# A two-layer decoder on one core: the context's keys and values of the second attention are computed during the recurrent mixer

## The chip, the cores and the metric

One core of a Trainium2 chip runs the whole program in one launch. The metric is device time in microseconds (us) of that core, the median of several executions. TensorE (PE in the profile, with PEld for its weight loads) multiplies and transposes, VectorE (DVE), ScalarE (ACT) and GpSimd (POOL) do the rest, SyncE (SP) only issues transfers (DMAs). Each engine works off its own queue in order; a semaphore wait at the head of a queue holds everything behind it. Everything is 32-bit float but a few counting steps.

## The reference

`x` and `ctx_1024` have 16 sequences of 128 rows, 256 wide. Two layers, each of mixer, attention over the context, mixture of experts, each with a residual and a plain layer norm:

```python
x = _layernorm(x + L0_attn(x))              # state space mixer
x = _layernorm(x + L0_xattn(x, ctx, ctx))   # 16 heads of 16
x = _layernorm(x + L0_ffn(x))               # 16 banks, 2 per row
x = _layernorm(x + L1_attn(x))              # recurrent mixer (wkv) with its own gated feed-forward
x = _layernorm(x + L1_xattn(ctx, x))        # 8 heads of 64, below
x = _layernorm(x + L1_ffn(x))               # 32 experts, 6 per row, one shared, 16 anchors
```

The second attention is the one changed:

```python
xn = layer_norm(ctx, gamma_x, beta_x);  ln = layer_norm(x, gamma_l, beta_l)
q = (ln @ Wq) * 64 ** -0.5
k_x, v_x = split(xn @ Wkv);  k_l, v_l = split(ln @ Wkv)
k = concat([rope_rotate_k(k_x), k_l]);  v = concat([v_x, v_l])
out = softmax(q k^T) v @ Wo                 # per sequence and head: 128 queries, 256 keys
```

What the change moves is `xn`, `k_x` (with the rotation) and `v_x`: they depend on the context alone.

## The kernel before, in words

`X` holds the residual stream, a batch (one sequence) on 128 partitions by 256. `Engine` objects T, V, A, G, S record the queue of each engine; a call's `w=` puts waits on handles ahead of it. `Slots` is a ring of buffers, each with the handles that free it; `ps` is the ring of the 8 PSUM banks. A part of the kernel is a generator that yields where another part's instructions may come in between. `pipeline` starts one generator per step and advances every live one by one segment in each step, the oldest first; so the order in each engine's queue is fixed at build time.

Stages, in order: state space mixer; first attention (16 batches in groups of four, `pre_c` making queries, keys and values of a group, `post_c` closing it, the function `fill` called three times a batch to advance them); first routing; 47 tiles of experts (`tile0`, 41 of them always); the recurrent mixer (`phase_e`, 8 units of two batches); second attention; second routing spread through it; experts and anchors; the final sum.

- `comb0(u)`, the head of `phase_e(u)`: four gathers by GpSimd of expert rows, two batches' sums on VectorE, a layer norm. Segment by segment a unit then does: scale and affine, the three mixes (VectorE), three projections, two scans and a reciprocal of 512 (VectorE), an output projection, a layer norm, the feed-forward of 1024 (TensorE), two layer norms. A unit takes 13 steps; the unit that runs step 6 has the scans.
- `fill_zeros` issues, on SP's queue, one of 50 blocks of zeros of some 2.2 MB into the destinations `xs` and `xsa` of the second routing, with three lanes, so that SP stops at a block until the third before it has landed. 24 are issued in the first attention; the mixer issues the other 26, up to four calls a unit. `place`, deep in the second attention, waits for all.
- `pre_f(g)`: loads the context of four batches on SP's queue (`in_ctx`), scales `x` on ScalarE and turns it into `lt`, then layer norm of the context (bn_stats on VectorE, a power on GpSimd, ScalarE applies it), turns it (8 transposes) into the other half of `lt`; then queries and the keys of `x`, one 512-wide product pair per segment.
- `keys_f(g, b)`: keys of the context (two 512-wide products), the rotation (two VectorE products out of PSUM, one GpSimd sum), values of context and of `x` (two products each, copies on ScalarE), then four transposes of the keys and a copy on ScalarE.
- `half_f(g, b, hf)` does the scores, maximum, exponential, transposes and values of four heads; `post_f` the output projection and the routing (`choose_f`, `place`: 7 scatters by GpSimd per batch, two between yields). Items come in the order `keys_f` of the next batch, half 0, `post_f` of the last, half 1, with `pre_f` of the next group in each group's first batch.
- The arena (53,200 columns of each partition) is laid out anew per stage; barriers stand between stages.

## Time and profile before

| | us |
|---|---|
| median of 3 runs | 1767.93 |
| lowest, highest | 1762.32, 1769.79 |
| profiled execution, its own time | 1781.69 |
| its span (first to last instruction) | 1779.9 |

| engine | busy us | share of the span |
|---|---|---|
| PE | 1437.8 | 81% |
| DVE | 846.7 | 48% |
| ACT | 571.7 | 32% |
| POOL | 516.8 | 29% |

The mean granted clock of TensorE is 0.903 of full speed. Busy time is a mean over stages with different limits; in the trace the first attention lies at 160 to 340 us, the first experts at 398 to 694, the recurrent mixer at 696 to 976, the second attention at 977 to some 1430, its last part routing alone.

### The profile page before, as it was taken

To read this page: it belongs to the slowest core of one execution; us is meant where nothing else is said; L and a number is where in the kernel's file an instruction comes from. 1 tells how busy PE (TensorE), PEld (TensorE's weight loads), DVE (VectorE), ACT (ScalarE), POOL (GpSimd) and SP (SyncE) were. 2 spreads that over 40 slices of the span, in tenths; PEclk is the share of its full clock that TensorE was granted. 3 is DMA by queue.
4 is the path that set the end of the run, shared out by engine and by line. 5 is a ranking of instruction groups with operands and counts; after the bars stand their busy time and mean duration, and the time that the engine had idled before them with its cause. 6 is when DMAs were issued, how large, how long until landed. Compare 5 with 4: busy or idle time off the path is not lost.

```text
span 1779.9 us, 30995 instructions
## 1 busy us (share of the span) xinstructions
PE 1437.8 (81%) x11425; PEld 1145.6 (64%) x11425; DVE 846.7 (48%) x2403; ACT 571.7 (32%) x1448; POOL 516.8 (29%) x524
## 2 busy tenths in 40 slices
PE   8567888649999997568997789978886467999878
PEld 4454676539999996346886356645555245888767
DVE  6254565451112222698852145555675433555534
ACT  3222322222222221123222254555454212555520
POOL 1011000011111102444443001034255634556544
PEclk9898999769999998678999799999997767999989
DMA  7745776649888881999999100011012596455456
GB/s 168 116 159 183 316 287 275 266 148 375 331 325 327 330 322 65 198 224 224 214 213 212 33 13 1 13 37 48 25 60 70 224 345 215 148 150 151 143 207 239
DMA packets 154926, 329.22 MB, mean 185 GB/s; under 512 B 11936, under 2 KB 118064, under 8 KB 149264
## 3 DMA queue, kind: packets, MB, share of 16 engines
q1 hardware_dynamic: 135424, 277.34, 51.6%
q0 software_dynamic: 15888, 43.52, 7.0%
q10 hardware_dynamic: 3456, 6.29, 1.1%
q8 instruction: 94, 1.54, 0.4%
q14 instruction: 64, 0.52, 0.1%
HBM read 174.51 MB, written 152.60 MB: 184 GB/s over the span
## 4 chain that ended last, share of the span: by engine, by line
PE 50%; DVE 12%; issue 5%; ACT 5%; POOL 4%; DMA 4%; DVEq 0%; SPq 0%; ACTq 0%; another core or an unknown queue 0%; POOLq 0%
PE bank L153 50%; DVE arena L153 11%; ACT arena L153 5%; POOL arena L153 3%; POOL xs L153 1%; DMA arena<-ys,arena 1%; DMA arena<-in_bank 1%; DMA arena<-xsa 1%; DMA arena<-in_ctx 1%; DVE arena L130 0%; DMA arena<-in_banka 0%; DMA xs<-arena 0%; DVEq L129 0%; POOL xsa L153 0%; DMA arena<-ys 0%
## 5 line engine op out<-in xcount | busy, mean ns | idle before, releaser
L153 PE MATMUL bank<-arena 128*128 128x128 f32 (+11 forms) x11425 | 1437.8, 326 | 336.1 <-DVE arena L153 151.7
L153 PEld LDWEIGHTS bank<-arena 128*128 128x128 f32 (+7 forms) x11425 | 1145.6, 175 | 628.0 <-issue 239.4
L153 ACT ACTIVATE arena<-bank 128x512 f32<-128x512 f32 (+3 forms) x627 | 267.5, 465 | 637.5 <-PE bank L153 591.9
L153 POOL TENSOR_TENSOR arena<-arena 128x512 f32<-128x512 f32 (+5 forms) x180 | 176.7, 982 | 719.3 <-DVE arena L153 563.1
L153 ACT ACTIVATE arena<-bank,arena 128x256 f32<-128x256 f32 (+3 forms) x486 | 204.0, 455 | 233.0 <-PE bank L153 154.4
L153 DVE TENSOR_TENSOR arena<-bank,arena 128x128 f32<-128x128 f32 (+5 forms) x331 | 123.8, 388 | 177.7 <-PE bank L153 101.6
L153 DVE TENSOR_SCALAR arena<-bank,arena 128x128 f32<-128x128 f32 (+1 forms) x212 | 69.7, 384 | 268.5 <-PE bank L153 268.5
L153 ACT ACTIVATE arena<-arena 128x256 f32<-128x256 f32 (+9 forms) x203 | 107.5, 586 | 270.5 <-DVE arena L153 244.8
L153 POOL DMA_INDIRECT ys<-arena x146 | 152.2, 1043 | 135.6 <-ACT arena L153 84.3
L153 DVE COPY arena<-bank 128x256 f32<-128x256 f32 (+2 forms) x136 | 76.4, 579 | 141.8 <-PE bank L153 139.5
L153 DVE TENSOR_REDUCE arena<-bank 128x4 f32<-128x512 f32 (+1 forms) x128 | 81.0, 684 | 91.4 <-PE bank L153 91.3
L153 POOL DMA_INDIRECT xs<-arena x96 | 95.0, 989 | 64.8 <-ACT arena L153 33.1
L153 DVE SCALAR_TENSOR_TENSOR arena<-arena 128x1 int32<-128x1 f32 (+4 forms) x297 | 87.3, 314 | 51.0 <-POOL arena L153 16.9
L153 POOL DMA_INDIRECT arena<-xd,arena x41 | 38.8, 947 | 250.1 <-PE bank L153 219.7
L153 DVE TENSOR_TENSOR arena<-arena 128x512 f32<-128x512 f32 (+18 forms) x248 | 98.6, 422 | 6.0
L130 DVE COPY arena<-arena 128x768 f32 x114 | 65.1, 571 | 48.3 <-issue 28.8
L153 DVE TENSOR_SCALAR arena<-arena 128x2 f32<-128x2 f32 (+12 forms) x178 | 49.0, 278 | 25.2 <-POOL arena L153 18.1
L153 DVE BATCH_NORM_STATS2 arena<-arena 128x6 f32<-128x256 f32 x128 | 48.6, 419 | 11.9 <-DMA arena<-in_ctx 9.4
L153 DVE RECIPROCAL arena<-arena 128x4 f32<-128x4 f32 (+8 forms) x56 | 38.4, 686 | 26.5 <-ACT arena L153 24.2
L153 POOL DMA_INDIRECT arena<-ys,arena x32 | 33.5, 1048 | 8.8 <-issue 8.8
L153 DVE RECIPROCAL arena<-bank 128x256 f32<-128x256 f32 x16 | 28.1, 1755 | 14.3 <-PE bank L153 14.3
L153 ACT ACTIVATION_READ_ACCUMULATOR arena<-bank,arena 128x1 f32 x128 | 26.1, 204 | 0.0
(22 smaller groups left out, 146.5 us busy)
## 6 DMA issues: line engine op xcount, KB each, us to landing
arena<-in_bank SPq DMA_DIRECT2D x41, 2052.0 KB
xs<-arena SPq DMA_DIRECT2D x32, 2193.0 KB, 31.8
xsa<-arena SPq DMA_DIRECT2D x16, 2193.0 KB, 9.7
arena<-xs SPq DMA_DIRECT2D x114, 129.0 KB
arena<-ys SPq DMA_DIRECT2D x16, 896.0 KB, 6.8
arena<-in_bank SPq DMA_DIRECT2D x8, 1536.0 KB, 6.8
arena<-kd SPq DMA_DIRECT2D x16, 512.0 KB, 10.3
arena<-in_banka ACTq DMA_DIRECT2D x24, 256.0 KB
```

The lines of the kernel that those rows point to most:

```text
L130: eng.tensor_copy(out, src[:, bass.ds(at * size, size)]).then_inc(self.sem, 1)
L153: ins = fn(*a, **kw)
```

## The change

In the first attention each group's context, which is there anyway, is also normalised (without gamma and beta) and stored to a new tensor `cnd`. Near the end of the first experts a part `fetch` loads its first two pieces of 256 rows on ScalarE's queue. `context(u)`, 8 of them, turns a piece and makes rotated keys and values of its two batches in one buffer `ob` of 1024 columns; `turn_keys` transposes the keys, and stores the buffer (512 KB) to `kvd` from ScalarE's queue. The mixer's loop is written out: before the live units advance, `tick()` runs twice in steps 0 to 4 and once in later ones; one tick stands before the mixer's gathers. A tick starts a unit of context at every even count and advances the live ones. There are two buffers `ob` (in `XT`), so that a batch's rotation waits for the store of the batch two before. In the second attention `load_kv` fetches keys and values of a batch, two batches ahead, on SP's queue, and waits for all stores; `pre_f` and `keys_f` lose the context's part. The mixer's ring `mix` has 8 buffers instead of 9.

```diff
         def layernorm(src, dst, nb, w=(), act=False, again=None):
             V.wait(*w, *sw)
+            if act:
+                A.wait(*w)
...
+        def norm_c(g):
+            cb, hc = C[g]["ctx"]
+            nb, w = cnb.get()
+            V.wait(hc)
+            h = yield from layernorm(lambda b: cb[:, b * 256:(b + 1) * 256], lambda b: nb[:, b * 256:(b + 1) * 256], 4, w=w, act=True)
+            ctxb.put(cb, h, C[g]["turned"])
+            if g + 2 < 4:
+                load_c(g + 2)
+            yield
+            h_cn.append(S.dma(s.dma_start, cnd[512 * g:512 * g + 512, :].rearrange("(b t) f -> t b f", b=4), view(nb, 0, [[256, 4], [1, 256]]), nlane, w=[h]))
+            cnb.put(nb, h_cn[-1])
+            yield
...
             if pre and slot[0] % 3 != 2:
                 next(pre, None)
+            if slot[0] % 3 == 2:
+                next(norm, None)
...
+        def load_cn():
+            u = len(loaded)
+            if u < 8:
+                cb, w = cbuf.get()
+                loaded.append((cb, A.dma(a.dma_start, view(cb, 0, [[256, 2], [1, 256]]), cnd[256 * u:256 * u + 256, :].rearrange("(b t) f -> t b f", b=2), cnl[u % 2], w=[*h_cn, *w])))
+
+        def context(u):
+            cb, hc = loaded[u]
+            ct, cw = cnT.get()
+            for kc, bk, h in to_feature(lambda b, kc: cb[:, b * 256 + kc * 128:b * 256 + kc * 128 + 128], [hc], 2):
+                hl = A(a.activation, ct[:, kc * 256:kc * 256 + 256], bank(bk)[:, 0:256], ACT.Identity, scale=vcol("gx", kc), bias=vcol("bx", kc), w=[h, *cw])
+                ps.put(bk, hl)
+            cbuf.put(cb, h)
+            load_cn()
+            yield
+            for b in range(2):
+                ob, ow = kvo.get()
+                bk, bw = ps.get()
+                T.wait(hl, h_w[3], *h_late, *bw)
+                for kc in range(2):
+                    h = mm(bank(bk), ct[:, kc * 256 + b * 128:kc * 256 + b * 128 + 128], wcol("kv2", kc, 0, 512), kc == 0, kc == 1, sig=(kc == 1))
+                rb, rw = rope.get()
+                V(v.tensor_tensor, view(rb, 0, [[64, 8], [1, 64]]), view(bank(bk), 0, [[64, 8], [1, 64]]), view(cc("cos"), 0, [[0, 8], [1, 64]]), ALU.mult, w=[h, *rw, *ow], free=True)
+                h = V(v.tensor_tensor, view(ob, 0, [[64, 8], [32, 2], [1, 32]]), view(bank(bk), 32, [[64, 8], [-32, 2], [1, 32]]), view(cc("sin"), 0, [[0, 8], [32, 2], [1, 32]]), ALU.mult, free=True)
+                ps.put(bk, h)
+                hr_ = G(p.tensor_tensor, rb, rb, ob[:, 0:512], ALU.add, w=[h])
+                bk, bw = ps.get()
+                T.wait(*bw)
+                for kc in range(2):
+                    h = mm(bank(bk), ct[:, kc * 256 + b * 128:kc * 256 + b * 128 + 128], wcol("kv2", kc, 512, 512), kc == 0, kc == 1, sig=(kc == 1))
+                hv = A(a.activation, ob[:, 512:1024], bank(bk), ACT.Copy, w=[h, *ow])
+                ps.put(bk, hv)
...
+                turning.append((2 * u + b, ob, rb, hr_))
+                yield
+                turn_keys()
+            yield
+
+        def turn_keys():
+            n, ob, rb, hr_ = turning.pop(0)
+            bk, bw = ps.get()
+            T.wait(hr_, *bw)
+            for m in range(4):
+                h = tr(bank(bk)[:, m * 128:(m + 1) * 128], rb[:, m * 128:(m + 1) * 128], ident, sig=(m == 3))
+            rope.put(rb, h)
+            hk = A(a.activation, ob[:, 0:512], bank(bk), ACT.Copy, w=[h, hr_])
+            ps.put(bk, hk)
+            h_kv.append(A.dma(a.dma_start, kvd[128 * n:128 * n + 128, :], ob, kvl[n % 2], w=[hk]))
+            kvo.put(ob, h_kv[-1])
+
+        def tick():
+            if ticks[0] % 2 == 0 and ticks[0] < 16:
+                units.append(context(ticks[0] // 2))
+            ticks[0] += 1
+            units[:] = [c for c in units if next(c, "end") != "end"]
...
-        pipeline([tile0(i) for i in range(LIKELY0)])
+        pipeline([tile0(i) for i in range(LIKELY0 - 4)] + [fetch()] + [tile0(i) for i in range(LIKELY0 - 4, LIKELY0)])
...
+        tick()
         for e in (T, V, A, G):
             e.wait(*h_ys[-3:])
...
-        mix = Slots([alloc(512) for _ in range(9)])
+        mix = Slots([alloc(512) for _ in range(8)])
...
-        pipeline([phase_e(u) for u in range(8)])
+        live, todo, n = [], deque(phase_e(u) for u in range(8)), 0
+        while todo or live:
+            for _ in range(2 if n < 5 else 1):
+                tick()
+            if todo:
+                live.append(todo.popleft())
+            live = [e for e in live if next(e, "end") != "end"]
+            n += 1
...
         def pre_f(g):
-            hc = S.dma(s.dma_start, view(cb, 0, [[256, 4], [1, 256]]), cv[g], clane2[0], w=cw)
-            h = yield from layernorm(cg, cg, 4, w=[hc], act=True)
-            for kc, bk, h in to_feature(lambda b, kc: cb[:, b * 256 + kc * 128:b * 256 + kc * 128 + 128], [h]):
-                hl = A(a.activation, lt[:, 1024 + kc * 512:1024 + kc * 512 + 512], bank(bk), ACT.Identity, scale=vcol("gx", kc), bias=vcol("bx", kc), w=[h])
...
+        def load_kv():
+            n = len(got_kv)
+            if n < 16:
+                kv, w = KV.get()
+                got_kv.append((kv, S.dma(s.dma_start, kv[:, 0:1024], kvd[128 * n:128 * n + 128, :], clane2[n % 5], w=[*h_kv, *w])))
...
         def keys_f(g, b):
-            rb, rw = rp.get()
-            hr = G(p.tensor_tensor, rb[:, 0:512], rb[:, 0:512], rb[:, 512:1024], ALU.add, w=[h])
-            for src in range(2):
...
+            load_kv()
+            c["kv"], c["hkx"] = got_kv[4 * g + b]
+            yield
             for kc in range(2):
+                h = mm(bank(bk), lt[:, kc * 512 + b * 128:kc * 512 + b * 128 + 128], wcol("kv2", kc, 512, 512), kc == 0, kc == 1, sig=(kc == 1))
+            c["hv"] = A(a.activation, c["kv"][:, 1024:1536], bank(bk), ACT.Copy, w=[h, c["hkx"]])
...
-        items = [pre_f(0)] + [nothing() for _ in range(7)] + [keys_f(0, 0)] + [nothing() for _ in range(6)]
+        items = [pre_f(0)] + [nothing() for _ in range(3)] + [keys_f(0, 0)] + [nothing() for _ in range(4)]
```

## Rows read from the trace of the kernel before

**Rows 1.** Stretches: us, then busy (count) per engine, PE clock, DMA share, GB/s.
```profile
160.00:340.00 180.00, 146.69 (x2743) 117.61 (x2741) 102.54 (x214) 57.80 (x120) 10.11 (x6) 0.94 0.76 298
694.00:735.00 41.00, 14.59 (x37) 10.67 (x38) 20.08 (x54) 5.74 (x14) 24.05 (x29) 0.54 0.55 132
735.00:821.00 86.00, 52.64 (x206) 41.98 (x205) 75.59 (x143) 19.78 (x42) 39.33 (x39) 0.78 1.10 224
821.00:971.00 150.00, 145.46 (x689) 127.02 (x687) 87.19 (x171) 41.38 (x80) 64.38 (x64) 1.00 1.10 214
977.00:1035.00 58.00, 39.29 (x149) 20.81 (x150) 15.96 (x43) 21.91 (x50) 4.56 (x4) 0.79 0.12 31
1035.00:1378.00 343.00, 290.03 (x1854) 192.18 (x1854) 191.45 (x559) 170.92 (x445) 106.89 (x110) 0.92 0.10 34
1378.00:1430.00 52.00, 21.40 (x80) 10.93 (x78) 25.48 (x108) 11.71 (x20) 32.78 (x34) 0.70 0.57 211
```

**Rows 2.** Chain of waits, shares by line, for 735 to 821 and 1035 to 1378.
```profile
by line: DVE arena L153 77.0%; PE bank L153 10.5%; POOL arena L153 4.9%; issue 4.4%; ACT arena L153 3.2%; DVEq L140 0.2%
...
by line: PE bank L153 55.6%; DVE arena L153 22.8%; ACT arena L153 12.7%; issue 6.1%; POOL xsa L153 1.3%; POOL xs L153 1.2%; POOL arena L153 0.2%; ACTq L140 0.1%; DVEq L140 0.1%; POOLq L140 0.0%
```

**Rows 3.** Groups by shape, 977 to 1380: count, busy us, mean ns, idle before.
```profile
L153 PE MATMUL bank<-arena 128*128 128x512 f32 x320 | 156.2, 620 | 0.9 <-ACT arena L153 0.9
L153 ACT ACTIVATE arena<-bank 128x512 f32<-128x512 f32 x148 | 83.5, 601 | 117.9 <-PE bank L153 115.7 <-issue 1.8
L153 DVE TENSOR_TENSOR arena<-bank,arena 128x512 f32<-128x512 f32 x32 | 20.5, 683 | 3.4 <-PE bank L153 3.4
L153 POOL TENSOR_TENSOR arena<-arena 128x512 f32<-128x512 f32 x16 | 20.3, 1268 | 93.7 <-DVE arena L153 93.7
```

**Rows 4.** Timeline of PEld, head of second attention: start, us, [idle before].
```profile
996.91 0.34 PEld L153 LDWEIGHTS bank<-arena 128*128 128x128 f32 x1 [0.52 <-issue]
...
1001.01 0.19 PEld L153 LDWEIGHTS bank<-arena 128*128 128x128 f32 x1 [0.24 <-issue]
```

**Rows 5.** Timeline of PE in the second attention.
```profile
992.21 1.97 PE L153 MATMUL bank<-arena 128*128 128x128 f32 x8 [11.74 <-ACT arena L153]
...
1025.27 2.22 PE L153 MATMUL bank<-arena 128*128 128x128 f32 x16 [1.33 <-DVE arena L153]
...
1116.00 47.95 PE L153 MATMUL bank<-arena 128*128 128x128 f32 x286 [4.00 <-ACT arena L153]
```

**Rows 6.** Timeline of DVE: the context's statistics, and the mixer's first scan.
```profile
734.57 1.22 DVE L153 TENSOR_TENSOR_SCAN arena<-arena 128x512 f32<-128x512 f32 x1
...
986.65 1.41 DVE L153 BATCH_NORM_STATS2 arena<-arena 128x6 f32<-128x256 f32 x4 [9.43 <-DMA arena<-in_ctx]
```

**Rows 7.** Landing times: mixer's gathers 696 to 735, 735 to 800; then `in_ctx`.
```profile
DMA to landing us min/median/max: 2.7/5.6/8.8
...
DMA to landing us min/median/max: 8.1/9.1/10.2
...
DMA to landing us min/median/max: 3.8/5.0/9.3
```

**Rows 8.** SP's queue in the mixer, and the page's issues of `xs` (median landing last).
```profile
712.34 252.25 SPq L153 DMA_DIRECT2D xs<-arena  x24
...
xs<-arena SPq DMA_DIRECT2D x32, 2193.0 KB, 31.8
```

**Rows 9.** Timeline of POOL: first gather, third unit's first scatter, last scatter.
```profile
699.26 0.95 POOL L153 DMA_INDIRECT arena<-ys,arena  x1 [0.16 <-issue]
...
1334.74 1.27 POOL L153 DMA_INDIRECT xsa<-arena  x1 [1.24 <-ACT arena L153]
...
1428.01 0.96 POOL L153 DMA_INDIRECT xs<-arena  x1 [0.30 <-issue]
```

**Rows 10.** Groups by shape, first attention 160 to 340.
```profile
L153 ACT ACTIVATE arena<-arena 128x256 f32<-128x256 f32 x12 | 6.2, 588 | 10.3 <-DVE arena L153 10.3
L153 DVE BATCH_NORM_STATS2 arena<-arena 128x6 f32<-128x256 f32 x12 | 4.2, 414 | 0.1
```

More of the change, by code:

```diff
@@ L642, in pre_c @@
                 ps.put(bk, hct)
-            ctxb.put(cb, h)
-            if g + 2 < 4:
-                load_c(g + 2)
+            c["turned"] = h
             yield
@@ L856, in build @@
                 pre, slot[0] = (pre_c(g + 1) if g < 3 else None), 0
+                norm = norm_c(g)
             m, hm = maxima(g, b)
@@ L1062, in tile0 @@
             yield
-        pipeline([tile0(i) for i in range(LIKELY0)])
+        kvd = nc.dram_tensor("kvd", [2048, 1024], F32, kind="Internal").ap()
+        cbuf = Slots([arena[:, 48848 + 512 * i:49360 + 512 * i] for i in range(2)])
+        cnT = Slots([arena[:, 49872 + 512 * i:50384 + 512 * i] for i in range(2)])
+        kvo, rope = Slots([]), Slots([])
+        cnl, kvl = [Lane(sem()) for _ in range(2)], [Lane(sem()) for _ in range(2)]
+        h_kv, loaded, turning = [], [], []
+        def load_cn():
[3 more added lines that the diff above has]
+                loaded.append((cb, A.dma(a.dma_start, view(cb, 0, [[256, 2], [1, 256]]), cnd[256 * u:256 * u + 256, :].rearrange("(b t) f -> t b f", b=2), cnl[u % 2], w=[*h_cn, *w])))
@@ L1065, in build, with fetch @@
+        ticks, units = [0], []
+        def tick():
[3 more added lines that the diff above has]
+            units[:] = [c for c in units if next(c, "end") != "end"]
+        def fetch():
+            yield
+            load_cn()
+            load_cn()
+        pipeline([tile0(i) for i in range(LIKELY0 - 4)] + [fetch()] + [tile0(i) for i in range(LIKELY0 - 4, LIKELY0)])
         with where_more(counts[0:1, 0:1], LIKELY0, NT0, r["hn"]):
@@ L1123, in build @@
         th = Slots([alloc(512) for _ in range(2)])
+        for i in range(2):
+            kvo.put(XT[:, 2048 + 1024 * i:3072 + 1024 * i])
+            rope.put(alloc(512))
         none = alloc(ROWX)
+        assert top[0] <= 48848
         V(v.memset, none, 0.0, free=True)
@@ L1309, in build @@
         oT2 = Slots([alloc(512) for _ in range(2)])
-        clane2 = [Lane(sem())]
+        clane2 = [Lane(sem()) for _ in range(5)]
         F = [dict() for _ in range(4)]
@@ L1397, in half_f @@
             c, f = FB[4 * g + b], F[g]
-            q, keys = f["q"], ((c["kx"], 128, 0), (f["kl"], 512, b * 128))
+            q, keys = f["q"], ((c["kv"], 128, 0), (f["kl"], 512, b * 128))
             m_, mw = sm.get()
@@ L1410, in half_f @@
             if hf:
-                kx.put(c["kx"], *hs)
                 if b == 3:
@@ L1457, in half_f @@
             if hf:
-                V2.put(vb, h)
+                KV.put(c["kv"], h)
                 c["ot"], tw = oT2.get()
@@ L1611, in post_f @@
                     yield
-        items = [pre_f(0)] + [nothing() for _ in range(7)] + [keys_f(0, 0)] + [nothing() for _ in range(6)]
+        for _ in range(2):
+            load_kv()
+        items = [pre_f(0)] + [nothing() for _ in range(3)] + [keys_f(0, 0)] + [nothing() for _ in range(4)]
         last = None
```

57 lines of the change are left out of this document (17 added, 40 removed).

## The prediction, made before the result was known

> **What bounds the kernel now.** I read first the stretches of time [rows 1]: they tell which engine is full where the change takes from and where it puts. In the second attention (1035 to 1378) PE is busy 290 of 343 us; in the mixer's second half (821 to 971) 145 of 150 at full clock. In the mixer's first half (735 to 821) DVE is busy 76 of 86 and PE 53, at a granted clock of 0.78; ahead of that (694 to 735) PE works 15 of 41 us at 0.54. So the room is in the mixer's first 125 us, and the second half has none. The chain of waits says the same [rows 2]: 77% DVE in 735 to 821; in the second attention 56% PE, 23% DVE and 13% ACT, so that PE work removed there isn't all time. Last, the timeline of POOL: it scatters from 1334.7 to 1429 with hardly a pause, while PE ends its last attention work near 1378 [rows 9]; whatever the last blocks gain is kept by the scatters. And the DMA engines are full through the mixer (share 1.10, 214 to 224 GB/s, against 34 in the attention) [rows 1].
>
> **What is moved, in TensorE time.** A batch's context costs 4 products of 512 columns (two for keys, two for values) and 4 transposes; a group 8 transposes more. The trace has each product as two records (320 where the code has 160) [rows 3]; from one weight load to the next are 0.43 us at full clock and 0.86 at half [rows 4]. A product is then 0.86 or 1.72 us. Transposes: 16 in 2.22 us at full clock, 8 in 1.97 at half [rows 5], 0.14 and 0.25 each. Sum: 64 x 0.86 + 96 x 0.14 = 68 us at full clock. DVE moves 32 rotations of 0.68 (22 us), POOL 16 sums of 1.27 (20 us), ACT 32 copies of 0.60 (19 us) [rows 3], each to the same number of instructions in the mixer.
>
> **Second attention, head.** The statistics of the first context wait 9.4 us for its load and start at 986.65 [rows 6]. PE has turned `x` by 980.5, then stands idle for 11.7 and turns the context in 2.0 [rows 5]; the products come only behind that. After the change they need the turned `x` alone: 13.7 us earlier. In front of the first scores two key and value pairs (3.4 us), 4 transposes and their waits also go, about 5. Saved: 18, if the first keys are there (see below).
>
> **Second attention, body.** Per group 4 x (3.44 + 0.56) + 1.1 = 17 us of PE go. In the ten steps with `pre_f` PE runs without a gap (48 us from 1116 [rows 5]); about 2.5 batches' keys and the context's transposes lie there, 11 us, and they go whole: what is left (37 us in ten steps, 3.7 a step) is more than the exponential and maximum ask per step on ACT and DVE (171 and 191 of 343 us, half of each [rows 1]). In the other seven steps PE's gaps are for DVE and ACT; of 6 us of PE there I count 2.5, and 1.5 for two copies and two rotations less in front of other work, 4 together. A group: 15. Groups 0 and 1 count whole, the third up to its third batch (12): 42. From there POOL's scatters bind; they lose only their sums of 1.27, and ACT and DVE hold them a little less: 5. Body 47, bounds: 30, if only the full-PE stretches give, to 68, all of the PE time less nothing. `load_kv` issues run two batches ahead of their use, some 40 us, against landings of 3.8 to 9.3 for as many bytes [rows 7]: no cost. Together 65 us less (48 to 85).
>
> **First attention.** `norm_c` adds per group 4 statistics of 0.41, small steps, a power on POOL, and 4 ACT passes of 0.59 [rows 10]: about 2.7 us DVE, 2.4 ACT, placed after the powers of every batch. PE is busy 147 of 180, DVE 103, ACT 58 [rows 1]. DVE is needed for the next maxima only after PE has made them, so most is hidden: 4 us in all (0 to 20, the upper end is all of it on the path). The later load of context g+2 still has some three batches of time. `fetch` and the tick ahead of the gathers stand beside full weight loads and the wait for the last stores: 0.
>
> **Mixer, steps 0 to 4, two ticks each.** Before, they took from 696.2 to the first scan at 734.6 [rows 6], 38 us, mostly waiting for gathers. I put the ticks into the queues one by one. In step 0 the keys' product (3.4 us at half clock, or 1.7), rotation 1.4, POOL's sum 1.3, then the same for the second batch stand ahead of the gathers on POOL: they start near 707 to 710, not 699.3 [rows 9], 10 late. In each later step: a transpose and copy, store issue, product, rotation; the second tick's rotation waits for the store issued in the first, since there are two buffers. PE needs 8.5 us a step (17 at half clock), the store 4 to 9, as `in_ctx` of the same bytes [rows 7], so a step is some 11 to 13 us against 7.7 before. In step 4 the fills stand beside it. Step 5 begins 28 us later: first scan near 763 (bounds +12, if the work fits the gathers' waits, to +50, if PE stays at half clock).
>
> **Steps 5 to 10, one tick each.** A step is about 20 us here and DVE's. A tick adds rotations of 1.4 and up to 1 of waiting for the product: five of them, 11 us; the products lie in PE's gaps, and PE's own products on the chain speed up with the clock (0.78 to 1.00), back 3. The last two batches fall into the full-PE half: 2 x 4 = 8. Sum 16 (5 to 25). Buffers: the store of a batch has a whole step of 20 us before its buffer is wanted. `mix` with 8 holds two steps of four: 0. Mixer together +44 (20 to 75).
>
> The price of a store beside the fills is the unknown. The gathers, 128 KB, land in 5.6 us with few fills and in 9.1 among them [rows 7]; the fills in 31.8 [rows 8] at 2193 KB, three in flight. A store of 512 KB is therefore between 9 and 32; I take 11. The Trainium skill (DMA: Bandwidth & Descriptors, Queues, rings and completion order) says that a DMA engine goes round between the queue rows that have work, one packet of each. By that rule the store on ACT's queue would have half of the engines' time beside SP's fills, an estimate of 5 us for 512 KB at 107 GB/s, and no wait in step 4 would reach DVE; that the gathers take 9.1 for a quarter of the bytes speaks against so little.
>
> **Fills and the first keys.** SP issues fills from 712 to 965 [rows 8], almost as long as the mixer; the context's load stands behind them and was waited for until 986.65 [rows 6]. After, the first is 26 late, and some 6.5 MB more share the engines (25 us at 215 to 330 GB/s): landed near 1034, the mixer done near 1020. The first keys are wanted about 12 us after that; 3 us of waiting (0 to 15).
>
> **Sum**, on the profiled execution: +4 +44 +3 -65 = -14 us of 1781.7, 1767.7. That execution is 13.8 above the median, which I take to stay: 1754.
>
> **Rivals.**
> - *Two buffers stall VectorE (slower).* If a store needs over some 16 us among the fills, the second tick of steps 3 and 4 waits it out, and in steps 5 to 10 the rotation, at the head of DVE's queue, holds the scans. Place: the wait on `ow`. At 24 us: 2 x 13 in steps 3 and 4, 6 x 2.5 later, 41 more: +27, 1795. For it: 31.8 for a fill, DVE 88% busy. Against: a step of 20 us lies between. 0.20.
> - *The second attention is held by ACT, DVE and POOL (no change).* Then it gives 47, not 65: 1772. For it: 36% of its chain is DVE and ACT. Against: 48 us of PE without a gap. 0.15.
> - *The first keys come late (no change).* The load stands on SP behind the last fills: if the stores slow these by twice what I count, another 15 us pass before the first scores: 1769. This is the change not freeing the head as it says. 0.07.
> - *The idle PE takes it nearly free (much faster).* Mixer +25, attention -78, the rest as above (+7): 1722 after the same 13.8. For it: 26 idle us of PE in the first 41, and half a clock to win. 0.10.
>
> **Numbers.** Forecast 0.48. A measurement of this kernel can't tell less than about 0.5% (9 us). Faster 0.48 + 0.10 = 0.58; same 0.15 + 0.07 = 0.22; slower 0.20. The likeliest's own range is 1735 to 1762, from the terms' middle parts; with the other cases up to one in ten on either side, 1722 to 1788.
>
> **What would show it.** First scan after the fences at 58 to 70 us from the mixer's start (38 before); full-PE half longer by 8 to 10; second attention's first scores 23 us after its start, not 43; body near 290 us to the third unit's scatters; scatters ending about 95 us after that unit starts; DVE waiting for a DMA of `kvd` in the mixer would be the first rival. Wrong I am if the mixer grows by over 70 or under 25, or the attention shrinks by under 48.

## The result: slower, and the profile after

The changed kernel takes 1785.9 us (median of 4 runs, 1775.2 to 1788.0), the kernel before 1765.1 (4 runs, 1760.5 to 1769.8): a ratio of 1.0105, with a 95% interval of 1.0054 to 1.0157, so some 19 us slower (21 by the medians). The forecast was 14 us less. The profiled execution of the changed kernel is 1786.7 us, its span 1784.9.

To see where the time went I cut each profile at the same marks: the first attention's memset, the first wait for the experts' weights, the mixer's memset, the mixer's first 128x512 scan, SP's load of `wd`, the first scatter to `xsa` of units 0, 1 and 2, and the last scatter to `xs`. Each number is the us from one mark to the next. "First att." is the first attention, "MoE" the first experts, "start" the mixer up to its first scan; "head+1st" runs to the first scatter of unit 0, "2nd" and "3rd" to those of units 1 and 2, and "tail" to the last scatter.

```
kernel             first MoE   mixer: scans| second attention:            | all of it | after
                   att.        start       | head+1st  2nd   3rd   tail   | (4)       | it
before             264.5 297.3  38.3  242.1|  200.1    96.9  61.1  93.3   |   451.4   | 351.9
before_again       264.8 297.3  36.9  243.0|  192.3    98.3  60.1  91.4   |   442.1   | 353.2
after              271.6 300.6  72.6  252.4|  164.7    85.0  64.9  91.1   |   405.7   | 343.9
norm_only          270.5 298.8  37.2  241.8|  192.0    98.1  67.0  91.3   |   448.5   | 354.1
attention_only     264.3 297.3  36.7  241.0|  163.0    87.1  62.1  92.6   |   404.8   | 356.3
mixer_only         269.1 298.5  73.5  255.2|  192.3    99.5  64.7  93.6   |   450.2   | 350.0
pad_products       269.4 300.8  76.0  252.5|  184.6    90.6  62.2  91.9   |   429.3   | 324.2
late_turn          270.2 300.8  73.4  255.2|  165.0    82.8  55.6  92.8   |   396.2   | 318.7
gathers_first      267.4 298.6  66.8  256.7|  164.7    84.9  58.5  91.7   |   399.7   | 319.0
both               270.6 300.6  67.5  255.8|  163.1    82.5  52.1  92.5   |   390.2   | 322.0
before_late        261.0 297.1  37.8  242.5|  201.7    85.8  56.2  93.7   |   437.3   | 344.3
half_moved         266.0 298.5  43.4  245.9|  171.5    97.4  66.8  91.5   |   427.2   | 349.8
half_moved_late    266.5 299.3  44.9  246.1|  162.3    86.5  54.0  92.9   |   395.7   | 347.4
quarter_moved_late 261.4 298.8  39.8  241.4|  175.9    86.9  54.3  93.1   |   410.3   | 351.6
later_ticks        269.7 301.9  64.4  289.1|  163.3    86.9  62.5  92.4   |   405.1   | 342.7
later_both         268.1 298.3  64.6  288.6|  164.5    88.0  56.7  94.2   |   403.4   | 343.8
later_room         271.8 300.6  62.2  288.8|  163.2    87.0  62.2  92.0   |   404.5   | 353.2
split_ticks        269.6 298.6  53.4  275.7|  162.8    86.9  62.5  90.8   |   403.0   | 341.3
split_late         268.1 299.4  53.9  275.8|  162.1    86.9  58.8  91.8   |   399.6   | 344.7
```

The stretch ahead of the first attention lies between 130 and 147 us with no order in it, and the last one is some 30 us shorter on the chip of pad_products, late_turn, gathers_first and both; both are left out of what follows. A second profile of the kernel before (before_again) stands in the table because the first has a late load in the head (below). Against it the change costs 10 us ahead of the mixer (7 and 3), 45 in the mixer (36 and 9), and saves 36 in the second attention: +19, which is what the ratio says. That match is partly chance: the attention of before took 442 to 451 us in the four profiles that have it (before, before_again, norm_only, mixer_only), so the saving is 36 to 46, and before_again is at its lower end. The two whole profiles lie only 2 us apart, since the stretches left out were 7 and 9 us shorter in the changed kernel's.

The stretches of the changed kernel, columns as in [rows 1]; the first answers to its 160 to 340, the next three to 694 to 821, then the head and the third group:

```profile
165.00:345.00 180.00, 145.22 (x2692) 116.30 (x2696) 106.75 (x236) 62.67 (x130) 13.09 (x10) 0.94 0.79 310
708.00:745.00 37.00, 29.53 (x98) 14.74 (x99) 14.05 (x28) 11.33 (x22) 19.61 (x21) 1.00 0.39 132
745.00:783.00 38.00, 30.95 (x98) 17.59 (x97) 20.18 (x49) 11.86 (x24) 18.31 (x19) 0.87 0.65 189
783.00:880.00 97.00, 71.70 (x278) 51.67 (x278) 86.44 (x155) 26.88 (x56) 46.35 (x43) 0.88 1.09 266
1036.00:1090.00 54.00, 47.48 (x211) 26.66 (x212) 14.86 (x27) 21.99 (x55) 0.55 (x1) 0.90 0.17 61
1285.00:1349.90 64.90, 45.22 (x320) 34.07 (x320) 33.87 (x109) 30.39 (x83) 29.60 (x31) 0.82 0.16 58
```

In the mixer's start PE is now busy 29.5 of 37 us at full clock, where it was 14.6 of 41 at 0.54. The idle PE was there and was used, and still the stretch grew from 38 to 73 us. The last line is the third group of the attention. It has 36 matmul records less than in the kernel before and takes no less time. The same group in before_again and in norm_only, which both have the attention of before:

```profile
1277.89:1338.04 60.15, 50.67 (x356) 34.26 (x356) 38.18 (x115) 33.45 (x89) 33.55 (x34) 0.95 0.18 63
```
```profile
1269.76:1336.75 66.99, 55.12 (x356) 37.03 (x356) 38.15 (x115) 33.42 (x89) 33.21 (x34) 0.88 0.16 56
```

With the same instructions it takes 60 or 67 us, and the granted clock is 0.95 or 0.88; in the changed kernel it is 0.82. The two differ in one place, where the same work of PE has the full clock once and a lower one the other time (before_again, then norm_only); ahead of it they need 31 and 32 us and behind it 10.3 both:

```profile
1309.06:1327.76 18.70, 15.07 (x119) 9.91 (x119) 15.06 (x45) 10.11 (x27) 8.19 (x9) 1.00 0.12 44
```
```profile
1301.74:1326.47 24.73, 19.54 (x118) 12.70 (x119) 15.03 (x45) 10.10 (x27) 7.90 (x9) 0.79 0.09 33
```

The whole second attention, from SP's load of `wd` to the last scatter, in before_again and in the changed kernel:

```profile
987.33:1429.48 442.15, 349.50 (x2076) 223.50 (x2076) 232.65 (x708) 205.15 (x515) 143.47 (x147) 0.89 0.15 53
```
```profile
1035.33:1440.99 405.66, 296.75 (x1852) 198.34 (x1852) 203.44 (x636) 176.09 (x459) 119.37 (x127) 0.84 0.21 73
```

The 224 records that are gone are the work that the forecast put at 68 us of PE at full clock. PE's busy time fell by 53 of them: the rest, some 15, stands beside a lower clock (0.84 against 0.89) and is an estimate. PE's idle time grew from 93 to 109 us, by 16. What is left of the 53 is the saving, 36.

PE at the mixer's start of the changed kernel, then its first gather on POOL and its first scan on DVE (start, us, what it waited for), against [rows 6, 9]:

```profile
726.66 9.61 PE L153 MATMUL bank<-arena 128*128 128x128 f32 x32 [1.88 <-POOL arena L153]
738.19 9.61 PE L153 MATMUL bank<-arena 128*128 128x128 f32 x32 [1.93 <-POOL arena L153]
...
720.58 0.97 POOL L153 DMA_INDIRECT arena<-ys,arena  x1
...
782.95 1.21 DVE L153 TENSOR_TENSOR_SCAN arena<-arena 128x512 f32<-128x512 f32 x1
```

A step with two ticks is 9.61 us of PE and 1.9 of waiting for POOL's sum: 11.5, and PE has no more gaps to give. The issues of the fills and the stores (KB each, median us to landing), the landing of the stores alone, of those issued before 757 us (the first fill is issued at 757.61) and of those issued from 785 on, then SP's first loads for the second attention:

```profile
xs<-arena SPq DMA_DIRECT2D x32, 2193.0 KB, 28.8
kvd<-arena ACTq DMA_DIRECT2D x16, 512.0 KB, 4.3
...
DMA to landing us min/median/max: 2.6/2.8/3.7
...
DMA to landing us min/median/max: 8.8/9.5/9.9
...
1035.33 0.35 SPq L153 DMA_DIRECT2D arena<-in_wd  x1
1036.22 2.24 SPq L153 DMA_DIRECT2D arena<-kvd  x5
```

The median of 4.3 us mixes two cases: a store lands in 2.6 to 3.7 us ahead of the fills and in 8.8 to 9.9 beside them. The fills land in 28.8 against 31.8 before [rows 8]. In this profile no DVE wait in the mixer is for a `kvd` store; that of pad_products, with the same mixer, has one of 8.6 us.

### The profile page after: what moved, and what is told of

The parts are those of the page before. It is cut to its first block, busy times and chain, and to the rows that moved or that the text cites. A ratio compares the mean times of both kernels' runs of the same rounds, so it can differ in the third digit from the quotient of the medians.

```text
span 1784.9 us, 31125 instructions
## 1 busy us (share of the span) xinstructions
PE 1449.7 (81%) x11425; PEld 1154.3 (65%) x11425; DVE 852.0 (48%) x2403; ACT 578.8 (32%) x1456; POOL 517.2 (29%) x524
## 4 chain that ended last, share of the span: by engine, by line
PE 33%; DVE 12%; POOL 5%; issue 5%; ACT 3%; DMA 2%; DVEq 0%; ACTq 0%; SPq 0%; another core or an unknown queue 0%; POOLq 0%
PE bank L153 33%; DVE arena L153 11%; POOL arena L153 4%; ACT arena L153 3%; DMA arena<-in_banka 1%; DMA arena<-xsa 1%; DVE arena L130 1%; POOL ys L153 0%; POOL xs L153 0%; DVEq L129 0%; DMA arena<-ys 0%; DMA ys<-arena 0%; ACTq L117 0%; POOL xsa L153 0%
## 5 line engine op out<-in xcount | busy, mean ns | idle before, releaser
L153 PE MATMUL bank<-arena 128*128 128x128 f32 (+10 forms) x11425 | 1449.7, 329 | 329.3 <-DVE arena L153 152.1
L153 PEld LDWEIGHTS bank<-arena 128*128 128x128 f32 (+6 forms) x11425 | 1154.3, 177 | 624.3 <-issue 248.4
L153 ACT ACTIVATE arena<-bank 128x512 f32<-128x512 f32 (+2 forms) x627 | 270.6, 465 | 686.7 <-PE bank L153 639.4
L153 DVE SCALAR_TENSOR_TENSOR arena<-arena 128x1 int32<-128x1 f32 (+5 forms) x297 | 87.7, 317 | 30.0 <-POOL arena L153 15.7
L153 DVE TENSOR_SCALAR arena<-arena 128x256 f32<-128x256 f32 (+14 forms) x178 | 52.3, 296 | 26.2 <-POOL arena L153 18.2
L153 POOL DMA_INDIRECT xsa<-arena x16 | 16.0, 999 | 39.8 <-ACT arena L153 18.9
## 6 DMA issues: line engine op xcount, KB each, us to landing
xs<-arena SPq DMA_DIRECT2D x32, 2193.0 KB, 28.8
```

The source lines that it names most:

```text
L153: ins = fn(*a, **kw)
```

## Experiments

Ratios are to the kernel before on the same chip, with 95% intervals.

### The parts of the change

**attention_only** leaves the first attention and the mixer as before; its second attention is the changed one, and in place of the context's keys and values it loads rows of `bank0`, so those data are not the context's, and the second routing differs. Ratio 0.9775 (0.9728 to 0.9823).

```
- S.dma(..., kvd[128 * n:128 * n + 128, :], clane2[n % 5], w=[*h_kv, *w])
+ S.dma(..., ins["bank0"][128 * n:128 * n + 128, 0:1024], clane2[n % 5], w=w)
```

> Only the second attention is changed: keys and values of the context are loaded per batch, but from a bank of finite weights, so that the attention's result and the second routing differ; first attention and mixer are as before. The prediction's sizes: 65 us less. My theory now (a half's turn waits for its own product, and the products removed were what TensorE did in that time): 40 to 50 us less, and a group of four batches takes some 86 us, not 80; in it TensorE waits for DVE some 2.7 us per half. Rival (all of TensorE's removed time comes back, and the loss is in the stages ahead): 60 or more less.

**mixer_only** has the changed first attention and mixer and the second attention of before: 1.0359 (1.0312 to 1.0407).

```
  # after's head and mixer, then before's pre_f, keys_f and buffers
+ A.wait(*h_kv)
+ V.wait(*h_kv)
```

> The context's keys and values are made in the mixer and stored, and the second attention makes its own as before (it does not read the stored ones). If the prediction's sizes for first attention and mixer hold: 48 us more. By the two traces, which differ by 10 ahead of the mixer and 45 in it: 50 to 58 more. Rival, that the traces' difference ahead of the mixer is chance of one execution: 44 to 48.

**norm_only** has the norm of the context in the first attention and its stores, and besides these only the mixer's ring of 8 buffers instead of 9: 1.0042 (1.0012 to 1.0073). **before_again** is the kernel before once more: 1784.5 us. The cut shows norm_only against the changed kernel.

```
- pipeline([tile0(i) for i in range(LIKELY0 - 4)] + [fetch()] + [tile0(i) ...])
+ pipeline([tile0(i) for i in range(LIKELY0)])
...
- for _ in range(2 if n < 5 else 1):
-     tick()
```

> The first attention also normalises and stores the context, nothing else is changed and nothing reads what is stored. Predicted 4 us more. By the two traces the first attention's stretch is 5.8 us longer: 4 to 8 more. If the 14 us by which the changed kernel enters the mixer late all come from here: 10 or more.

> The kernel before once more, for a second profile: how far stretches of the same kernel differ from one execution to the next. If the 9 us by which the last stage of the changed kernel was shorter are chance, this profile's last stage (from the last scatter to the end, 351 us in the first) is shorter as well, 342 to 346, and its mixer and attention agree with the first within 3 us.

By the medians the attention's part is worth 40 us and the other part costs 61: the sum is the change. mixer_only came out above its whole expected range: its stretches have 6 us ahead of the mixer and 49 in it (before_again), and its attention is 8 above before_again's with the same instructions. The attention takes the same 405 us alone as in the changed kernel. So the saving is not lost to a late store, a late load or the fills: it is small where it is made. The norm is 6 us in the first attention, not 4. before_again missed what was expected of it too: its last stage took 353 us, not 342 to 346, so the 9 us there are not shown to be chance by it, and its attention is 9 us shorter than the first profile's.

Of these 9, 8 lie in the head. The second group of PE transposes of the context (start, us, what PE waited for) in before_again and in before_late, and DVE's statistics in both:

```profile
997.28 1.97 PE L153 MATMUL bank<-arena 128*128 128x128 f32 x8 [6.14 <-ACT arena L153]
...
991.72 1.41 DVE L153 BATCH_NORM_STATS2 arena<-arena 128x6 f32<-128x256 f32 x4 [3.83 <-DMA arena<-in_ctx]
```
```profile
988.90 1.97 PE L153 MATMUL bank<-arena 128*128 128x128 f32 x8 [13.16 <-ACT arena L153]
...
983.34 1.40 DVE L153 BATCH_NORM_STATS2 arena<-arena 128x6 f32<-128x256 f32 x4 [10.85 <-DMA arena<-in_ctx]
```

How late the load of the context comes varies between executions: 3.8 us of waiting in before_again (3.7 in norm_only, 3.4 in mixer_only), 9.4 in the profile I forecast from [rows 6], 10.9 in before_late.

### What the removed products had been covering

**pad_products** puts two idle pairs of key products (four products of 512 columns, whose result nobody reads) back into each batch of the changed attention, by the forecast's price some 55 us of PE: 1.0303 (1.0229 to 1.0377).

```
  c["kv"], c["hkx"] = got_kv[4 * g + b]
+ idle_pair(g, b)
  yield
+ idle_pair(g, b)
```

> The changed kernel, and in the second attention each batch again makes four products of 512 columns whose result nobody reads (the product time that the change took away, 64 x 0.86 = 55 us, without rotations, copies and transposes). If TensorE's time is what the attention gives back (the prediction's step), all 55 come on top: near 1840. If TensorE has idle time there, since each half's turn waits for its maximum, exponential and product, and the clock falls in the gaps, then 10 to 30 come on top: 1795 to 1815, and the wait of TensorE for DVE shrinks.

**late_turn** leaves the removed products out and gives the turn of the powers (the transposes of a half's exponentials) one more step of distance; the output product goes to the end of the step: 1.0076 (1.0033 to 1.0120). **before_late** has the same two edits in the kernel before: 0.9918 (0.9881 to 0.9955).

```
      sm.put(m_, hn)
      yield
+     yield
      turned = []
...
- blocks.insert(2, post_f(*last) if last else nothing())
+ blocks.append(post_f(*last) if last else nothing())
```

> The changed kernel with one step more between a half's product and its turn, and the projection of the last batch entered one place later; the same instructions. If the chain of one half holds the second attention, the next half's scores now stand in that wait: 15 to 35 us less than the changed kernel, TensorE's waits for DVE mostly gone. If TensorE, ACT or POOL were the bound: within 5 us of it, since no instruction goes.

> The kernel before with late_turn's two edits to the second attention and nothing moved. My theory (PE's waits for one half's exponential come from the products taken away, which had been the cover): with the products there the edits give little, 0.997 to 1.001. Rival (the order of turn and output product costs in both kernels alike): the same 5 to 10 us as in the changed kernel, 0.994 to 0.997, and then late_turn's gain says nothing on the moved work.

The 55 us of products cost 24 in the attention (by the ratios the time is some 35 longer, above the 10 to 30 expected), 20 of them in the head and first group, 6 in the second and none later: beyond the first group PE had most of the time. What PE waits for there, one half batch of the changed kernel shows. DVE, ACT and PE (start, us, wait):

```profile
1122.92 1.29 DVE L153 TENSOR_REDUCE arena<-bank 128x2 f32<-128x512 f32 x2 [1.86 <-PE bank L153]
1125.61 0.18 DVE L153 RECIPROCAL arena<-arena 128x4 f32<-128x4 f32 x1 [0.89 <-ACT arena L153]
1125.83 1.29 DVE L153 TENSOR_TENSOR arena<-arena 128x512 f32<-128x512 f32 x2
...
1123.65 0.47 ACT L153 ACTIVATE arena<-bank,arena 128x256 f32<-128x256 f32 x1 [1.57 <-DVE arena L153]
1125.01 0.48 ACT L153 ACTIVATE arena<-bank,arena 128x256 f32<-128x256 f32 x1
...
1126.57 5.09 PE L153 MATMUL bank<-arena 128*128 128x128 f32 x44 [2.66 <-DVE arena L153]
```

From the maximum at 1122.92 to the turn on PE at 1126.57 a half goes through DVE, ACT (four exponentials) and DVE again: 3.7 us in which PE has what stands between in its queue, here 1.0 us, and waits the other 2.66. Fewer products make that chain no shorter. PE's waits from the second stretch of the attention to the third unit's first scatter (us in total, times, longest) in before_again, after, pad_products, late_turn, before_late and half_moved_late:

```profile
PE bank L153 <- ACT arena L153: 21.4, 8, 5.7
PE bank L153 <- DVE arena L153: 12.8, 13, 2.5
```
```profile
PE bank L153 <- DVE arena L153: 38.5, 15, 4.8
PE bank L153 <- ACT arena L153: 19.3, 11, 3.2
```
```profile
PE bank L153 <- DVE arena L153: 23.4, 13, 3.1
```
```profile
PE bank L153 <- ACT arena L153: 29.9, 13, 5.5
PE bank L153 <- DVE arena L153: 21.1, 5, 6.5
```
```profile
PE bank L153 <- DVE arena L153: 4.8, 3, 2.8
```
```profile
PE bank L153 <- ACT arena L153: 26.5, 11, 4.3
PE bank L153 <- DVE arena L153: 4.9, 3, 2.5
```

The waits for DVE are 12.8 us with the products, 38.5 without and 23.4 with idle ones in their place; the 15 waits of the changed kernel are 2.6 us in the mean. late_turn was to give 15 to 35 us and gave 5 by the ratios, 9.5 in the attention: PE's waits for DVE fell from 38.5 to 21.1 us, and those for ACT rose from 19.3 to 29.9. So that PE stands idle more is measured; that one half's latency is what holds it is read off the timeline, and the test made for it freed little. My theory that late_turn's gain comes from the lost cover fell with before_late: the same edits save 12 us in its second group and 4 in its third (against before_again), 0.8% in all. The distance between powers and turn was too short in both kernels; the products had hidden part of that. Of the tail, 91 to 94 us in all kernels, no edit changed anything: that is what the scatters on POOL, with hardly a pause there [rows 9], lead one to expect.

### The mixer's start

**gathers_first** moves POOL's sum to DVE and the ticks behind the mixer's segments: 1.0119 (1.0063 to 1.0175). **both** is that with late_turn: 1.0059 (1.0022 to 1.0096).

```
- hr_ = G(p.tensor_tensor, rb, rb, ob[:, 0:512], ALU.add, w=[h])
+ hr_ = V(v.tensor_tensor, rb, rb, ob[:, 0:512], ALU.add)
...
+ for _ in range(2 if n < 5 else 1):      # now behind the line `live = [...]`
+     tick()
```

> The changed kernel with the context's rotation summed on VectorE instead of GpSimd, and the ticks behind the mixer's segments in each step instead of ahead. If the mixer's first steps are long because gathers and context work hold each other in one chain through GpSimd's queue (gathers behind sums, products behind sums), the first scan comes 10 to 20 us earlier than 72.6 after the mixer's start, and the time falls by 8 to 18. If it is TensorE's work (5 units of 8.5 to 17 us) or the stores: within 4 us of the changed kernel, with sums on VectorE costing 0.7 each.

> late_turn and gathers_first together. If each frees a chain of its own, the gains add: 25 to 50 us below the changed kernel, which is 5 to 30 below the kernel before. If the routing's scatters then bind the attention's end, late_turn's part shrinks: at the kernel before's time.

The start gives back 6 us, where 10 to 20 were expected, and the scans take 4 of them: the time is that of the changed kernel, as the rival had it. both was to be 25 to 50 us under the changed kernel and is some 8 under it. Of the mixer's 45 us the order of the gathers was the small part.

### How much to move

**half_moved** moves the work of groups 0 and 1 only, one tick a step; groups 2 and 3 make theirs in the attention. **half_moved_late** is that with late_turn's edits, **quarter_moved_late** moves group 0 alone. All three also have four instead of five buffers `sb` for the exponentials; what that costs by itself no run shows.

```
- norm = norm_c(g)
+ norm = norm_c(g) if g < 2 else skip_c(g)     # 1 in quarter_moved_late
- for _ in range(2 if n < 5 else 1):
+ for _ in range(1):
...
  lt = F[g]["lt"]
+ if g >= 2:
+     yield from made_here(c, lt, g, b)        # products and turns as before
+     return
```

> Only groups 0 and 1 (8 batches) have their context's keys and values made in the mixer, one turn a step; groups 2 and 3 make theirs in the second attention as the kernel before did, and the norm of the context in the first attention is made for two groups alone. With late_turn's two edits. My theory (moved work is worth its cost in the head and in the first group, and little after it, where one half's scores, maximum and exponential set the turn): mixer some 20 to 25 us over before instead of 45, first attention 3 over, head and first group 28 less, second group 10 to 12 less, the third and fourth as before: 0.985 to 0.998 of the kernel before. Rival (the saving is spread evenly over the groups, so half moved gives half of it, and the mixer takes half of its cost): half of late_turn's difference to before, 1.000 to 1.005.

> half_moved_late without the late turn and with the output product back at its place. Theory: the late turn gives 8 to 11 us in the second and third group whether products stand beside or not (before_late gave 11 and 4 there), and the half that is moved gives its 28 to 38 in the head against 10 in the mixer and 3 in the first attention: 0.985 to 0.992. Rival (the two edits need one another, since the late turn's cover is what lets the head go on): 0.998 to 1.004.

> Only group 0 (4 batches) is made in the mixer; groups 1 to 3 make theirs in the second attention, the norm is moved for group 0 alone; with late_turn's edits. If the gain lies in the head and belongs to the work of group 0 and the first half of group 1 (theory: what stands there in front of the first turns): mixer 3 to 6 us over before, head to the first gathers 20 to 30 less, the later groups as in half_moved_late: 0.978 to 0.988, some 10 us less in the mixer and 5 to 15 more in the head than half_moved_late. Rival (what counts is the total of products taken from the attention): half of half_moved_late's gain over before_late, 0.986 to 0.990.

half_moved_late: 0.9804 (0.9754 to 0.9854), medians 1744.0 us against 1773.2, the lowest ratio of a kernel that does the whole work. quarter_moved_late: 0.9834 (0.9799 to 0.9869), which the intervals don't tell apart from it. half_moved: 0.9983 (0.9959 to 1.0008), as its rival had it: the edits need one another. The table says why. Moving one group costs nothing in the mixer (281 us against 280) and saves 16 to 26 in the head (against before_again and before_late). The second costs 10 in the mixer and 5 in the first attention and saves 14 in the head, even. The third and fourth cost 36 to 38 more in the mixer; with the late turn they save nothing at all (attention 396 in half_moved_late and in late_turn), without it 21, of them 12 in the second group's stretch. Half of the move and the late turn together save 31 us more in the attention than half of the move alone.

### Two ticks in one step

**later_ticks** has two ticks in steps 4 to 8 instead of 0 to 4: 1.0202 (1.0158 to 1.0245). **later_both** adds late_turn: 1.0252 (1.0213 to 1.0290). **later_room** is later_ticks with a third output buffer and six buffers `mix` instead of eight: 1.0270 (1.0236 to 1.0304). **split_ticks** is later_ticks with the second tick in the middle of the step's segments: 1.0109 (1.0033 to 1.0185), **split_late** that with late_turn: 1.0133 (1.0060 to 1.0206).

```
- for _ in range(2 if n < 5 else 1):
+ for _ in range(2 if 4 <= n < 9 else 1):           # later_ticks
...
- mix = Slots([alloc(512) for _ in range(8)])
+ mix = Slots([alloc(512) for _ in range(6)])       # later_room
+ kvo.put(alloc(1024))
...
+ for i, e in enumerate(live):                      # split_ticks
+     if i == len(live) // 2 and 4 <= n < 9:
+         tick()
```

> The steps of keys' work are spread otherwise over the mixer: one a step in steps 0 to 3, two in steps 4 to 8, one after; the attention as after. My theory (the mixer's start is bound by PE, some 9.6 us of PE in a step with two turns of filling, while no scan runs yet): the stretch from the mixer's start to its first scan falls from 72.6 us to about 55, the stretch of scans rises from 252 to about 259, so the time is some 10 us under the changed kernel's, 1.000 to 1.004 of the kernel before. Rival (filling is paid once wherever it stands, since PE is the bound in all steps): the two stretches keep their sum of 325 us and the ratio stays at 1.010.

> later_ticks and late_turn in one kernel. If the two gains have nothing in common, 10 us and 5 to 10 us under the changed kernel: 0.993 to 1.000 of the kernel before. If what the mixer's start gave is paid in the scans, as in late_turn: 1.005.

> later_ticks with a third output buffer for keys and values (and six instead of eight buffers of the mixer's mixed inputs, to make room). If the two buffers are what cost 12 us a step in steps 4 to 8 (VectorE waits for the store's landing, TensorE then 15 us for GpSimd's sum): these steps fall from 35 us to 27 or less, no wait for a store of the keys, the mixer 353 -> about 320, ratio 1.000 to 1.005. If TensorE or GpSimd is the bound with two turns in a step: 33 to 35 us a step remain, the waits move to another engine, ratio 1.016 to 1.020.

> later_ticks, but in steps 4 to 8 the second turn of keys' work stands in the middle of the mixer's segments instead of right behind the first. Theory (TensorE's wait is for a sum that waits in VectorE's queue; half a step of other products covers most of it): these steps take 26 to 30 us instead of 34.7, PE's wait for GpSimd in the mixer falls from 66 us to 30 or less, the mixer from 353 to 320 to 335, ratio 1.002 to 1.011. Rival (VectorE or TensorE is full with two turns, 20 us of DVE and 24 of PE in a step of 24): the steps stay over 32 us, ratio 1.016 to 1.022.

> split_ticks with late_turn's edits. All 16 batches moved, the turns spread: if split_ticks' theory holds, 0.994 to 1.004; that would still be over half_moved_late's 0.980, since the products of groups 2 and 3 cost their TensorE time in the mixer and are worth nothing where they were. Under 0.985 would say that they are worth moving after all.

Both theories of later_ticks missed: the start fell by 8 us and the scans grew by 37. DVE's and PE's waits in its mixer, then PE, DVE and POOL around one of them:

```profile
DVE arena L153 <- DMA kvd<-arena: 44.0, 5, 9.1
...
PE bank L153 <- POOL arena L153: 65.5, 10, 15.4
...
833.27 19.29 PE L153 MATMUL bank<-arena 128*128 128x128 f32 x68 [15.39 <-POOL arena L153]
...
828.38 1.28 DVE L153 TENSOR_TENSOR arena<-bank,arena 128x512 f32<-128x512 f32 x2
...
830.97 0.95 POOL L153 DMA_INDIRECT arena<-ys,arena  x1 [0.30 <-issue]
831.95 1.27 POOL L153 TENSOR_TENSOR arena<-arena 128x512 f32<-128x512 f32 x1
```

I took the first line for the cause: DVE waits for a store, the forecast's first rival. With a third buffer that wait is gone and PE's is not (67.4 us, longest 15.4), and the mixer takes 351 us against 353, so it was a symptom; the two `mix` buffers fewer leave a remainder of doubt. The order in the queues explains the lines above. The second tick's turn follows the first tick's products at once in PE's queue; its sum waits for DVE's two rotations, which stand behind the scan's work (828.38), and then behind POOL's gathers (831.95). With half a step of other products between, in split_ticks, PE's wait is

```profile
PE bank L153 <- POOL arena L153: 19.0, 10, 4.5
...
PE bank L153 <- DVE arena L153: 26.5, 3, 9.1
```

and the mixer falls from 353 us to 329. Part of the wait has only changed its name: for DVE it was 2.7 us in later_ticks. And 329 is no better than the changed kernel's 325; DVE still waited 15.1 us for stores, in two waits. For a whole move the mixer pays some 45 to 49 us in either place. The late turn did not help where all is moved in the later steps: later_both was expected at 1.005 or less and split_late at 0.994 to 1.004, and they came out at 1.0252 and 1.0133, no faster than their kernels without it.

## Why the prediction was wrong

- **Ahead of the mixer**, +4 forecast, +10 measured: 6 in the first attention for the norm, the rest there and in the experts' stretch, where the fetch and the tick stand, which I had put at 0. Inside the bounds, too low. That fetch and tick cost anything is not shown: in norm_only, without them, that stretch is 1.5 us longer than in before_again, in mixer_only, with them, 1.2.
- **The mixer**, +44 forecast, +45 measured: 36 in its start and 9 in the scans, where I had 28 and 16. Right in the sum by luck: the parts missed by 8 and 7 in opposite directions. The first gather came 10.3 us after the mixer's memset (3.0 before), 7 late where I had 10; a step took 11.5 us, inside my 11 to 13, but by PE (9.6, and 1.9 for the sum) and not by a store, and at a clock of 1.00, where I had left open 0.5.
- **The stores.** I took 11 us for one; beside the fills it is 8.8 to 9.9. Ten of the 16 are issued ahead of them or with the first four, where the landings that the profile has took 2.6 to 5.0 us. The Trainium skill (DMA: Bandwidth & Descriptors, Queues, rings and completion order) has the engines go round between the queues that have work, which gave an estimate of 5 us: the trace of after does not bear this estimate out, with 9.5 in the median beside the fills, and my reading of the gathers' 9.1 us was the better guide. The rival of the two buffers, 0.20, wanted over 16 us for a store, and its wait is absent in the changed kernel's profile, one of 8.6 us in pad_products. In later_ticks DVE waits 44.0 us for stores, and the time is not theirs.
- **First keys late**, 3 forecast, 0 measured: SP issues them 0.9 us after the stage's first load, and the head is within 2 us as short with stores and fills as in attention_only (164.7 and 163.0).
- **The head.** It and the first group were to give 18 and 15, 33 together; they gave 35 against the profile of the forecast and 28 against before_again. The late load of the context is most of the difference between the two: I took 9.4 us from one execution for a property of the kernel [rows 6]; in three others it is 3.4 to 3.8, in a fourth 10.9. The first maximum comes 25.0 us behind SP's load of `wd`, 45.0 in the first profile, 38.9 in before_again: the head gave 20 or 14, and the first group 15 or 14, as forecast.
- **The body: the step that failed.** "In the other seven steps ... of 6 us of PE there I count 2.5", and before it that what is left of PE "is more than the exponential and maximum ask per step on ACT and DVE". I compared busy times of engines and let nearly all of the removed PE time count. Second group 13 where I had 15, third nothing (2 less than norm_only, 5 more than before_again) where I had 12, tail 0 where I had 5: the terms that failed are the third group's and the tail's, 17 of the 47. In their place PE waits: 38.5 us for DVE where it was 12.8, 2.6 a time, at a half whose path from the maximum to the turn is 3.7 us long; and it runs at a lower clock, in the third group 0.82. There PE is busy 45.2 of 64.9 us, 5 less than in before_again, and idle 10 more. Head and body together gave 36 against before_again and 46 against the profile of the forecast, where I had 65 and 48 at the least. An attention that shrinks by under 48 was one of my signs of being wrong.
- **The base.** My sum was made on an execution 13.8 us over the median, and I let the same distance stand. Some 8 of those lay in the head that the change takes away. By the terms as measured (+10, +45, -36) it is +19.

The condition of the second rival, an attention held by the other engines, is the one that was met, from the third group on, and its 47 us were nearly the right term; I gave it 0.15. With it, the measured +10 and +45 and no late keys, the sum is a loss of 8.

What stays open: what sets the clock of the third group. It takes 60 to 67 us with the attention of before (before_again, before, mixer_only 64.7, half_moved 66.8, norm_only 67.0), 58 to 65 with the changed one (gathers_first, after), 52 to 59 with the late turn. So the gain there can't be told to better than some 5 us, and no run parts what the waits cost from what the lower clock costs.

## What to carry to other kernels

PE work that is removed from a stage is worth its time only where PE is what the others wait for; read which wait ends last in each step and how long one item takes through all its engines, not the engines' busy sums. Where work is moved into idle time, price the first part apart from the rest: here a quarter was free to place, and with the late turn it did as well as a half within the noise; the last half cost some 36 us in the mixer and brought nothing once the turn had its distance. And filler that waits on its own earlier part needs other work between the two in the same queue.

## What the runs showed of the hardware

The mixer's start went from a granted clock of 0.54 to 1.00 when PE was given work: 98 matmul records take 29.5 us there, and 37 had taken 14.6 [rows 1]. The third group's clock differs between kernels whose instructions there are the same, 0.95 and 0.88, which goes with 7 us of 60, and 6 of them lie in one stretch of 118 or 119 matmul records: 18.7 us at 1.00, 24.7 at 0.79. Stores of 512 KB on ACT's queue landed in 8.8 to 9.9 us beside fills of 2193 KB and in 2.6 to 3.7 ahead of them, and the fills were not slowed (28.8 us against 31.8). And one stage alone can differ between sets of runs: the last stretch took 319 to 324 us in the four kernels that ran on one chip, 341 to 356 in all others.
